# Cross-attention pair on one core: row maxima brought from a column to a row by two DMAs over DRAM instead of matmuls with the identity

## What is computed

```
layer 0: h = layernorm(x)*gamma + beta;  Q = h@Wq, K = ctx@Wk, V = ctx@Wv     (16 heads of 64)
         attn = softmax(Q K^T) * 64**-0.5;   x = x + (attn @ V) @ Wo + bo
layer 1: xn = rmsnorm(x)*norm_w;  q = xn@wq, k, v = ctx@wkv                   (16 heads of 32)
         rotate q and k by position, divide each by its norm
         attn = softmax(q k^T * sqrt(32));   x = x + (attn @ v) @ wout
```

## Time and profile before

| | us |
|---|---|
| median of three runs | 3528.63 |
| the profiled execution, its own time | 3533.39 |
| its span, first to last instruction | 3531.6 |
| PE, DVE, ACT, POOL busy | 3224.5, 2379.0, 1405.2, 488.7 |
| exponentials on ACT (L725), 1024 | 996.3 |
| adds of exponentials on DVE (L795), 768 | 960.0 |
| row maxima on DVE (L776), 512 | 625.4 |
| row-maximum matmuls on PE (L610), 1024 | 249.5 |

### The profile page before, as it was taken

How to read it: one execution, slowest core, us unless ns; L and a number is a source line. 1 busy time by engine, 2 the same in 40 slices (tenths; PEclk the granted TensorE clock), 3 DMA queues, 4 the chain that set the end, 5 groups by cost and what they waited for, 6 DMA issues and landing times.

```text
span 3531.6 us, 51117 instructions
## 1 busy us (share of the span) xinstructions
PE 3224.5 (91%) x20448; PEld 1631.8 (46%) x20448; DVE 2379.0 (67%) x2805; ACT 1405.2 (40%) x1728; POOL 488.7 (14%) x221
## 2 busy tenths in 40 slices
PE   5899998888999999979999999988899999989897
PEld 3445445444345444534435445454444545545441
DVE  3566667577666666658676666666777666666777
ACT  1333333445533333345543333334564333334554
POOL 1000002243010000224200000032420000003430
PEclk7999999999999999989999999999999999999999
DMA  3001000111120100010111100001011100100001
GB/s 100 11 21 25 23 21 18 41 34 34 30 56 25 24 18 20 21 49 25 32 42 44 31 17 21 25 13 56 18 35 42 55 17 21 28 20 13 26 14 35
DMA packets 178321, 105.88 MB, mean 30 GB/s; under 512 B 81452, under 2 KB 147116, under 8 KB 178088
## 3 DMA queue, kind: packets, MB, share of 16 engines
q1 hardware_dynamic: 178088, 102.60, 10.9%
HBM read 93.12 MB, written 9.42 MB: 29 GB/s over the span
## 4 chain that ended last, share of the span: by engine, by line
PE 73%; DVE 14%; issue 5%; ACT 4%; DMA 3%; SPq 1%; DVEq 0%; POOL 0%; ACTq 0%; POOLq 0%
PE o_acc L652 17%; PE work L678 13%; PE scores L640 12%; PE work L674 11%; PE work L698 9%; PE work L610 4%; DVE tile_max L776 4%; DVE acc L795 4%; PE work L692 3%; ACT probs L725 1%; DVE q_low L870 1%; DVE k_low L870 1%; ACT k_high L740 1%; DMA rows_dram<-recip_t 1%; ACT q_high L740 1%
## 5 line engine op out<-in xcount | busy, mean ns | idle before, releaser
L725 ACT ACTIVATE probs<-scores 128x1024 f32<-128x1024 f32 x1024 | 996.3, 1023 | 517.6 <-PE scores L640 484.9
L795 DVE TENSOR_TENSOR acc<-acc,probs 128x1024 f32<-128x1024 f32 x768 | 960.0, 1272 | 21.6 <-ACT probs L725 1.6
L776 DVE TENSOR_REDUCE tile_max<-work 128x2 f32<-128x1024 f32 x512 | 625.4, 1222 | 386.3 <-PE work L610 386.3
L652 PE MATMUL o_acc<-probs,v_tok 128*64 128x512 f32 (+1 forms) x4096 | 781.7, 616 | 0.1
L912 POOL TENSOR_TENSOR inv<-sumsq,power 128x16 f32<-128x16 f32 x64 | 231.9, 3624 | 2287.2 <-DVE sumsq L861 2287.2
L698 PE MATMUL work<-wo,o_sum 128*128 128x512 f32 x768 | 431.2, 649 | 32.4 <-issue 21.8
L640 PE MATMUL scores<-q_high,k_high 32*128 32x512 f16 (+1 forms) x2048 | 314.4, 400 | 71.3 <-DVE q_low L870 34.4
L610 PE MATMUL work<-k_high,q_high 64*128 64x512 f32 x1024 | 249.5, 480 | 102.4 <-DVE tile_max L776 82.7
L880 DVE TENSOR_TENSOR resid<-work,resid 128x512 f32<-128x512 f32 x384 | 261.5, 684 | 94.0 <-PE work L698 93.2
L652 PEld LDWEIGHTS o_acc<-probs,v_tok 128*64 128x64 f32 (+1 forms) x4096 | 165.6, 123 | 340.2 <-issue 296.1
L640 PE MATMUL scores<-q_high,k_low 32*128 32x512 f16 (+1 forms) x2048 | 309.5, 392 | 0.0
(11 more groups left out here) (74 smaller groups left out, 2779.8 us busy)
## 6 DMA issues: line engine op xcount, KB each, us to landing
recip<-rows_dram SPq DMA_DIRECT2D x380, 64.0 KB, 2.1
wq<-in_L_xattn_Wq_dram SPq DMA_DIRECT2D x32, 256.0 KB, 3.0
stage<-in_x_dram SPq DMA_DIRECT2D x8, 1024.0 KB, 7.3
resid<-in_x_dram SPq DMA_DIRECT2D x8, 1024.0 KB, 5.5
wo<-in_L_xattn_Wo_dram SPq DMA_DIRECT2D x32, 256.0 KB, 2.7
out_dram<-resid SPq DMA_DIRECT2D x8, 1024.0 KB, 4.3
wk<-in_L_xattn_Wk_dram SPq DMA_DIRECT2D x32, 192.0 KB, 2.6
wv<-in_L_xattn_Wv_dram SPq DMA_DIRECT2D x32, 192.0 KB, 3.1
```

The costliest lines, as they stand in the source:

```text
L652: mm = pe.matmul(o_acc[h * d:(h + 1) * d, :], v_tok[par][:, kt, h * d:(h + 1) * d], probs[:, unit_slot(t, n, kt, h // 2), h % 2, :], start ...
L725: act.activation(probs[:, no % RING, :, :], scores[:, unit_banks(t, n, kt, u), :], ACT.Exp, scale=(1.0, float(D1) ** 0.5 / QK_SCALE ** 2)[ ...
L776: dve.tensor_reduce(tile_max[:, qt, :, n:n + 1], work[:, 0:G0, :], AX.X, ALU.max, negate=True).then_inc(dve_freed, 1)
L795: dve.tensor_tensor(a[:, heads, :], before, probs[:, unit_slot(t, n, kt, u), :, :], ALU.add).then_inc(add_ok, 1)
```

## The change

The T entry issues nothing on PE and ACT any more and takes no bank. SP, at the entry's place in the plan, waits for neg_max, stores it to a new DRAM tensor shift_rows (two heads by 1024), waits for that store, and loads the 512 values of each head into partitions 0 and 64 of shift, whose other partitions are set to zero once at the start. neg_max and tile_max change their layout: heads outermost, no zero columns. So that each partition's four values are consecutive in DRAM, a maxima tile no longer holds 128 consecutive queries but every fourth one of the half: rowmax loads its stationary operand from q_high with a step of four elements. PE's scores wait for the second DMA (shift_in). DVE waits for the store of the half before (shift_out) when it writes neg_max. The identity in float32r goes away, with its cast.

```diff
--- before.py
+++ after.py
@@ -60,8 +60,8 @@
         self.banks, self.before = (), ()
 
 
-WORK = ("R", "T", "q", "k", "v", "kr", "qr", "kT", "qT", "den", "den_end", "out", "ct", "xt")
-ACT_FREES = ("T", "v", "den", "ct", "xt")
+WORK = ("R", "q", "k", "v", "kr", "qr", "kT", "qT", "den", "den_end", "out", "ct", "xt")
+ACT_FREES = ("v", "den", "ct", "xt")
 HIGHS = ("q", "k", "kT", "qT")
 
 
@@ -342,6 +342,8 @@
     def tiles_of(half):
         return slice(half * HT, (half + 1) * HT)
 
+    shift_rows = nc.dram_tensor("shift_rows_dram", (G0, S), F32, kind="Internal").ap()
+
     with ExitStack() as ctx:
         def sb(name, shape, dt=F32, scope=ctx):
             return scope.enter_context(nc.sbuf_tensor(name, shape, dt))
@@ -350,7 +352,6 @@
             return ctx.enter_context(nc.semaphore(name))
 
         ident = sb("ident", [P, P])
-        ident_r = sb("ident_r", [P, P], F32R)
         ones_r = sb("ones_r", [P, P], F32R)
         ones = [sb("ones_scaled", [P, D0]), sb("ones_plain", [P, D1])]
         cos = sb("cos", [P, TT, D1])
@@ -381,8 +382,8 @@
         recip = sb("recip", [P, HALF])
         den_t = sb("den_t", [P, G1, HT])
         recip_t = sb("recip_t", [P, G1, HT])
-        tile_max = sb("tile_max", [P, HT, G0, 2])
-        neg_max = sb("neg_max", [P, HT, P], F32R)
+        tile_max = sb("tile_max", [P, G0, HT, 2])
+        neg_max = sb("neg_max", [P, G0, HT], F32R)
         shift = [sb(f"shift{i}", [P, S], F32R) for i in range(2)]
         raw = [sb(f"raw_{n}", [P, TT, G1, D1]) for n in ("k", "q")]
         turned = [sb(f"turned{i}", [P, HT, G1, D1]) for i in range(2)]
@@ -431,6 +432,8 @@
         dve_freed = sem("dve_freed")
         high_ok = sem("high_ok")
         neg_max_ok = sem("neg_max_ok")
+        shift_out = sem("shift_out")
+        shift_in = [sem(f"shift_in{i}") for i in range(2)]
         scores_ok = sem("scores_ok")
         exp_ok = sem("exp_ok")
         add_ok = sem("add_ok")
@@ -551,8 +554,18 @@
                     row = h * g // G1
                     sp.dma_start(recip[h * D1:(h + 1) * D1, :], rows[1, row:row + 1, tokens(n)].to_broadcast([D1, HALF])).then_inc(recip_in, 16)
 
+            def send_shift(t, half):
+                no = 2 * turn0_no(t) + half + 1
+                sp.wait_ge(neg_max_ok, no)
+                with nc.allow_non_contiguous_dma("runs of four maxima"):
+                    sp.dma_start(shift_rows[:, tokens(half)].rearrange("h (p j) -> p h j", j=HT), neg_max[:, :, :].bitcast(F32)).then_inc(shift_out, 16)
+                sp.wait_ge(shift_out, 16 * no)
+                sp.dma_start(shift[t % 2][0:D0 + 1:D0, tokens(half)].bitcast(F32), shift_rows[:, tokens(half)]).then_inc(shift_in[half], 16)
+
             def entry(e):
-                if e.kind == "den":
+                if e.kind == "T":
+                    send_shift(e.t, e.i)
+                elif e.kind == "den":
                     send_sums(e.t, e.i)
                 elif e.kind == "recip":
                     send_recips(e.t, e.i)
@@ -607,7 +620,7 @@
                 par = e.t % 2
                 for h in range(G0):
                     r = slice(h * D0, (h + 1) * D0)
-                    mm = pe.matmul(work[:, h, :], high[0, "q", par][r, tile(half * HT + qt)], high[0, "k", par][r, tokens(n)],
+                    mm = pe.matmul(work[:, h, :], high[0, "q", par][r, half * HALF + qt:(half + 1) * HALF:HT], high[0, "k", par][r, tokens(n)],
                                    start=True, stop=True)
                 mm.then_inc(work_full, 1)
 
@@ -617,7 +630,7 @@
                     if l == 0:
                         wait_freed(pe, ITEM["k", t, 0])
                         wait_freed(pe, ITEM["q", t, n])
-                        wait_freed(pe, ITEM["T", t, n])
+                        pe.wait_ge(shift_in[n], 16 * (turn0_no(t) + 1))
                     else:
                         wait_freed(pe, ITEM["kT", t, 0])
                         wait_freed(pe, ITEM["qT", t, n])
@@ -676,10 +689,6 @@
                         for j in range(HT):
                             for c in range(n_c):
                                 mm = pe.matmul(w[:, tile(j)], src[:, c, tile(HT * e.i + j)], wt[:, c, :], start=(c == 0), stop=(c == n_c - 1))
-                elif e.kind == "T":
-                    pe.wait_ge(neg_max_ok, 2 * turn0_no(e.t) + e.i + 1)
-                    for j in range(HT):
-                        mm = pe.matmul(w[:, tile(j)], neg_max[:, j, :], ident_r[:, :], start=True, stop=True)
                 elif e.kind in ("kT", "qT"):
                     which = "kq".index(e.kind[0])
                     pe.wait_ge(scaled_ok, ITEM[e.kind[0] + "r", e.t, e.i].rope)
@@ -738,9 +747,6 @@
                 if e.kind in HIGHS:
                     act.wait_ge(work_full, e.full)
                     act.activation(high[TURN[e.t][1], e.kind[0], par][:, tokens(e.i)], w, ACT.Copy).then_inc(high_ok, 1)
-                elif e.kind == "T":
-                    act.wait_ge(work_full, e.full)
-                    act.activation(shift[par][:, tokens(e.i)], w, ACT.Copy).then_inc(act_freed, 1)
                 elif e.kind == "v":
                     act.wait_ge(work_full, e.full)
                     act.activation(v_tok[par][:, tiles_of(e.i), :].rearrange("p t d -> p (t d)"), w, ACT.Copy).then_inc(act_freed, 1)
@@ -773,10 +779,13 @@
                 if (n, qt) == (0, 0) and (e.t, half) != (0, 0):
                     dve.wait_ge(neg_max_ok, 2 * turn0_no(e.t) + half)
                 dve.wait_ge(work_full, e.full)
-                dve.tensor_reduce(tile_max[:, qt, :, n:n + 1], work[:, 0:G0, :], AX.X, ALU.max, negate=True).then_inc(dve_freed, 1)
+                dve.tensor_reduce(tile_max[:, :, qt, n:n + 1], work[:, 0:G0, :], AX.X, ALU.max, negate=True).then_inc(dve_freed, 1)
                 if (n, qt) == (1, HT - 1):
                     dve.wait_ge(dve_freed, e.dve)
-                    dve.tensor_reduce(neg_max[:, :, 0:D0 + 1:D0], tile_max[:, :, :, :], AX.X, ALU.min).then_inc(neg_max_ok, 1)
+                    no = 2 * turn0_no(e.t) + half
+                    if no > 0:
+                        dve.wait_ge(shift_out, 16 * no)
+                    dve.tensor_reduce(neg_max[:, :, :], tile_max[:, :, :, :], AX.X, ALU.min).then_inc(neg_max_ok, 1)
 
             def added(t, n, kt):
                 if kt == 0:
@@ -897,9 +906,9 @@
             dve.memset(ones[0][:, :], float(D0) ** 0.5)
             dve.memset(ones[1][:, :], 1.0)
             dve.memset(ones_r[:, :].bitcast(F32), 1.0)
-            dve.memset(neg_max[:, :, :].bitcast(F32), 0.0)
-            dve.wait_ge(ident_in, 16)
-            dve.tensor_copy(ident_r[:, :], ident[:, :]).then_inc(consts_ok, 1)
+            for i in range(2):
+                v = dve.memset(shift[i][:, :].bitcast(F32), 0.0)
+            v.then_inc(consts_ok, 1)
             dve.wait_ge(tables_in, 16 * 2)
             run(rowmax, lambda t, n, kt: None, added, entry)
 
```

## The result

The change makes the kernel slower: 3566.50 us (median of 4 runs, 3565.18 to 3567.21) against 3529.39 (4 runs, 3525.57 to 3534.49), ratio 1.0104 with a 95% interval of 1.0086 to 1.0121. That is +37.1 us where 15.8 fewer were forecast.

A forecast was written before the change was run, and what follows sets the result against it. PE was taken as the bound (busy 91%, 73% of the chain matmul time). Terms −43.0 (T off PE), +27.2 (four uncovered hops) and 0 (strided loads) gave −15.8: 3512.8 us against the median 3528.6, range 3498 to 3545.

The forecast's parts named there:

- Strided weight loads … I take 0: Row-maximum loads of every fourth query in layer 0: hidden under running matmul pairs, cost 0; upper bound 189 us.
- rival D: Strided row-maximum loads double to 0.37 us, 0.14 us exposed per pair: +72, net +56, 3584 us; chance 0.20.
- T off PE: T's matmuls leave PE and the denominators get bank 2: 0.87 us in each of 44 places, 43.0 us less together.
- rival E: Row-maximum pair still waits, for the residual add in bank 0: 30.7 saved, net −3.5, 3525 us; chance 0.06.
- the 0.21 us: Wait between T and the row-maximum pair until ACT's sums copy frees bank 1; claimed to vanish with T.
- The four uncovered hops: End of each (6,0) half: scores 5.0 us later plus 1.8 for the fallen clock, four times, 27.2 us cost.
- B: Rival on the four stalls: long, 10.7 us each, 42.8 in all, net −0.2, 3528.4 us; chance 0.11.
- C: Rival on the four stalls: short (1.55 + 1.67), no clock fall, 3.5 us each, net −29, 3499.6; chance 0.11.
- What is queued behind the wait loses 0.1 us at most: SP's queue beside other work: T's hops delay the reciprocals' store by 0.1 us at most; 12 us of cover.

The follow-up runs named there:

- s3: The changed kernel with consecutive weight loads and without the hops and their waits, so without any shift: 3483.49 us, 0.9873.
- s4: s3 with the strided weight loads of the changed kernel, still without hops: 3517.70 us, 0.9964.
- s2: The changed kernel with weight loads of 128 consecutive queries, all DMAs and waits kept: 3525.68 us, 0.9983.
- s5: The changed kernel with the weight loads put behind T(t7,0) in SP's order: 3545.12 us, 1.0041.
- s6: s5 with layer 0's other Ts moved from step 0 to step 1, behind the reciprocals' trip on SP: 3540.47 us, 1.0022.
- s10: The kernel before with T put ahead of the denominators, so that these get bank 2: 3518.48 us, 0.9953.
- s13: The changed kernel with step-two loads, first hop in runs of two maxima, T behind the reciprocals on SP, T(t7,0) back on PE and ACT: 3506.38 us, 0.9928.
- s7: The changed kernel with consecutive loads and the first hop as two DMAs of 512 single values: 4045.26 us, 1.1451.
- s11: The changed kernel with consecutive loads, single-value hops issued by GpSimd's queue, and T(t7,0) made by matmuls as before: 3772.61 us, 1.0679.

## Why the prediction was wrong

**The step that failed** is "Strided weight loads … I take 0". It measured +34.2 us without hops, +38.6 in before, +40.8 with hops: 0.07 to 0.08 us for each of 512 pairs, above the 0.05 from which rival D decides. So D came in, slower than before, with about half its price of 0.14 us a pair. Its load is shorter than supposed (305 ns, not 370), and its place is the opposite of what I argued. In the running stream of scores, where I looked, a pair stays at 0.23 and hides the load. The pair behind a full-array product (denominators, k, q or v products), whose loads nothing hides, pays the whole +0.12 us, the load's own difference (305 less 183 ns): 0.55 for 0.43. Where PE waits for DVE to free the banks, that wait swallows it (0.32 us in s3, 0.19 in s4), and the pair that starts behind the wait pays in its place: 0.50 at 1139.35 in s3, 0.62 at 1156.84 in s4, the same place. The regular half pays 0.48 (−0.83 in s3, −0.35 in s4), which is four of its eight pairs. I named the row of the exposed pair myself and priced the load from the hidden one. The Trainium skill's rule on lines, which the prediction named, was right here: 305 ns with one value on each line, 191 with two.

**T off PE** was right in kind. A regular half saves 0.83 to 0.85 where nothing else is touched (s3, s2), against 0.87: rival E, by which the 0.21 us would have stayed, is out. s3's −46.8 less its 8.9 at the four stall places leaves 37.9, against 43.0; by the two profiled executions alone (3531.6 and 3479.4) it is 43.3, so that gap is within their scatter. One term was too large: the three (0,1) halves gave 0.74 us together and not 3 × 0.87 (which wait took the rest back was not looked at).

**The four uncovered hops** were right. Net of T they cost 6.76 + 6.90 + 6.23 + 7.08 = 27.0 us, against 27.2, with some luck in the last digits, since part of this is the stride (with consecutive loads, s2, it is 25.3). In batch 1 hop 1 took 2.92 (3.0), hop 2 2.09 (1.67), the scores waited for shift 6.9 at the longest (6.4 forecast), and the low clock lasted 4 us (3.6). B and C are out. s5 shows that SP's order, not the weights' traffic, made over half of the stall, and that hop 1 takes 2.75 us even ahead of them; C's 1.55 was too low.

**"What is queued behind the wait loses 0.1 us at most"** failed as well, and it shows in the halves with the least slack. At the four stall places the hops cost 32.9 us (after's +27.0 against the −5.9 that s4 has there), so of the 48.8 about 15.9 lie elsewhere. The profiled executions of after and s4, which differ by 43.5, leave 10.6 for it: +9.9 in the (6,1) halves, +3.7 in the (0,1) halves of batches 2 to 4, −3.3 in (7,1), and next to nothing in the regular ones. At (6,1) of batch 1, SP's timeline of after and then of before:

```profile
594.76 0.49 SPq L540 DMA_DIRECT2D rows_dram<-sums  x1
596.34 0.37 SPq L544 DMA_DIRECT2D den_t<-rows_dram  x1
596.76 0.46 SPq L561 DMA_DIRECT2D shift_rows_dram<-neg_max  x1
598.42 0.49 SPq L563 DMA_DIRECT2D shift<-shift_rows_dram  x1
598.96 0.40 SPq L550 DMA_DIRECT2D rows_dram<-recip_t  x1
```

```profile
588.91 0.48 SPq L537 DMA_DIRECT2D rows_dram<-sums  x1
590.46 0.38 SPq L541 DMA_DIRECT2D den_t<-rows_dram  x1
592.96 0.36 SPq L547 DMA_DIRECT2D rows_dram<-recip_t  x1
```

and PE's chain there, after and then before:

```profile
602.95 2.71 issue
605.66 3.43 PE work L707 x4
```

```profile
597.68 1.23 issue
598.91 1.96 PE work L698 x4
```

The reciprocals' store is 2.62 us behind den_t's issue, not 2.50, just behind hop 2: here the 0.1 us as forecast. But PE already waited here for the reciprocals, so nothing is forgiven. From the sums' issue to the end of the attend blocks PE needs 8.19 us instead of 8.77, so T's 0.59 us turn into waiting. The reciprocals reach DVE 10.11 us after the sums' issue instead of 9.21. The wait grows from 1.23 to 2.71, and now the clock falls (0.57 in 605 to 609 us): the output products take 3.43 us instead of 1.96. The clock that a short delay tips was not priced. The delay itself was priced too low as well. By the median of the 41 regular halves the store goes 2.49 us behind den_t's issue in before, 2.98 in after (at most 3.92), but 1.93 in s3: with T off PE and no hop ahead of it the reciprocals are stored 0.56 us earlier. So the time of before was no measure of when SP would be wanted, and hop 1, whose wait took 1.58 to 4.49 us and not always 1.55, adds to it. In the regular halves all this is covered. In (6,1) of batch 4 the store goes 4.11 us behind den_t's issue (1.92 in before, 2.02 in s3), and the chain of after has

```profile
3223.40 3.55 issue
3226.95 3.50 PE work L707 x4
```

where before waits 0.55 us and takes 1.96. Part of that is den_t itself, which landed only 3.35 us after its issue beside hop 1. s6 moved the hops behind the reciprocals and removed about half of the loss in (6,1) and nearly all of it in (0,1); the rest stays open.

**The sum.** The four places +27.0 (+27.2 forecast), of which the stride has 3.0 (s4's −5.9 less s3's −8.9). Elsewhere T −37.9 (−43.0), the stride 34.2 − 3.0 = +31.2 (0), the hops +15.9 (0): +36.2, against −15.8 forecast and +37.1 measured. So of the 52 us that the forecast lacks, the stride is the largest part, 31.2, the hops at covered places are 15.9 and T is 5.1. The range ended at 3545; its upper part left out most of D's price.

## What to carry to other kernels

Price a new operand layout at the place in the chain where its load is exposed, not where it is hidden, and measure one load per step: two neighbouring values of 4 bytes a piece of 16 bytes were nearly free, one was 1.7 times the time. A wait that is put on a DMA queue is harmless only if the consumers of what is queued behind it have slack; look at the place with the least slack, and add the clock that a longer idle brings. Ask of a small operation on the critical engine first whether its order can change: s10 got a third of T's 46.8 us without touching the data path.

## What the hardware showed that I had not expected

- A weight load of 128 values of 4 bytes took 183, 191, 248 and 305 ns at steps of 1, 2, 3 and 4 values.
- A store from SBUF to DRAM took by the median 2.1 us to landing in runs of 16 bytes (after, one DMA of 4 KB), 3.6 in runs of 8 (s13, each of two DMAs of 2 KB) and 9.2 in runs of 4 (s7, each of two DMAs of 2 KB), the last by this row of the DMA issues (count, KB each, us to landing):

```profile
shift_rows_dram<-neg_max SPq DMA_DIRECT2D x128, 2.0 KB, 9.2
```

- Runs of 4 bytes slowed a small DMA of another queue while they lasted: the sums' store took 4.55 us instead of 1.55 (s11).
- PE's granted clock fell after short idles too, not only after the 8.16 us of the earlier trace rows: over windows of 4 us it was 0.57 behind an idle of 2.71 us (after), 0.58 behind 3.07 (s6) and 0.54 behind 3.25 (s5).
